# Cross-attention and quantised feed-forward on one core: the order of the work inside a tile's step

## The reference

```python
def _xattn(q1, key, value, weights, bias, drop_mask):   # key = value = ctx
    scores = jnp.einsum('bqd,bkd->bqk', q1, key) / 0.72
    attn = jax.nn.softmax(scores, axis=-1) * drop_mask
    o = jnp.einsum('bqk,bkd->bqd', attn, value) + bias
    return jnp.einsum('bqd,de->bqe', o, weights)

def _ffn(x, weight_q, weight_scale, bias):              # int8 weights, 512 x 512
    x_scale = jnp.maximum(jnp.max(jnp.abs(x), -1, keepdims=True), 1e-6) / 127.0
    x_q = jnp.clip(jnp.round(x / x_scale), -128, 127).astype(jnp.int8)
    acc = jax.lax.dot_general(x_q, weight_q, (((1,), (1,)), ((), ())), preferred_element_type=jnp.int32)
    return acc.astype(jnp.float32) * x_scale * weight_scale[None, :] + bias

x = x + _xattn(_layernorm(x), ctx, ctx, weights, attn_bias, mask)
x = x + _ffn(_layernorm(x), weight_q, weight_scale, ffn_bias)
```

## Time and profile before

| | before |
|---|---|
| median of 3 runs (lowest, highest) | 350.48 us (349.62, 350.58) |
| span of the profiled execution, first to last instruction | 348.8 us |
| PE busy | 332.0 us, 95% |
| DVE busy | 307.7 us, 88% |
| ACT busy | 239.0 us, 69% |
| POOL busy | 238.4 us, 68% |
| granted TensorE clock, mean | 0.998 |
| data moved | 43.74 MB, mean 125 GB/s |

### The profile page before, as it was taken

The page is one execution under the profiler, slowest core; times in us unless marked ns, Lnnn a source line. Parts: engine busy times, 40 slices in busy tenths (PEclk is TensorE's granted clock), DMA queues, the critical chain, the costliest instruction groups (busy, mean ns, idle before and its releaser), DMA issues. The chain is left out here.

```text
span 348.8 us, 6291 instructions
## 1 busy us (share of the span) xinstructions
PE 332.0 (95%) x1665; PEld 264.5 (76%) x1694; DVE 307.7 (88%) x630; ACT 239.0 (69%) x483; POOL 238.4 (68%) x368
## 2 busy tenths in 40 slices
PE   7999889999999999999999999999999999999993
PEld 7878667787777778777777787777778777787781
DVE  2687879989999999989999999989999999989887
ACT  3455787667777777677777667767776776777651
POOL 5163766778776777877777787867778787767643
PEclk9999999999999999999999999999999999999999
DMA  7949971634435173345516344552724341200002
GB/s 224 270 112 248 203 152 61 180 121 113 130 119 185 62 191 112 123 117 134 167 61 192 108 122 118 148 153 63 209 89 135 111 144 60 62 30 30 32 30 92
DMA packets 48226, 43.74 MB, mean 125 GB/s; under 512 B 3792, under 2 KB 34768, under 8 KB 48208
## 3 DMA queue, kind: packets, MB, share of 16 engines
q1 hardware_dynamic: 48208, 43.53, 44.6%
HBM read 35.13 MB, written 8.39 MB: 125 GB/s over the span
## 5 line engine op out<-in xcount | busy, mean ns | idle before, releaser
L1187 POOL TENSOR_TENSOR ct_lo<-ct_raw,ct_hi 128x512 fp32r<-128x512 f32 x28 | 36.3, 1296 | 29.3 <-ACT ct_hi L722 29.3
L744 ACT ACTIVATE x_norm<-x_blocks,norm_spread 128x128 f32<-128x128 f32 x124 | 51.2, 483 | 2.3 <-ACT norm_spread L737 1.5
L495 PE MATMUL ps_attn<-vw_hi,pt_hi 128*128 128x512 f32 x124 | 51.2, 413 | 0.1
L1139 POOL TENSOR_TENSOR scaled<-meanvar,scale 128x2 f32<-128x2 f32 x32 | 18.1, 564 | 46.6 <-DVE meanvar L900 46.6
L497 PE MATMUL ps_attn<-vw_hi,pt_lo 128*128 128x512 f32 x124 | 48.8, 394 | 0.0
L495 PE MATMUL ps_scores<-ct_hi,xt_hi 128*128 128x512 f32 x124 | 48.8, 393 | 0.0
L496 PE MATMUL ps_attn<-vw_lo,pt_hi 128*128 128x512 f32 x124 | 48.7, 393 | 0.0
L497 PE MATMUL ps_scores<-ct_hi,xt_lo 128*128 128x512 f32 x124 | 48.5, 391 | 0.0
L496 PE MATMUL ps_scores<-ct_lo,xt_hi 128*128 128x512 f32 x124 | 48.3, 390 | 0.0
L495 PE MATMUL ps_vw<-w_hi,ct_hi 128*128 128x512 f32 x116 | 48.2, 415 | 0.0
L497 PE MATMUL ps_vw<-w_hi,ct_lo 128*128 128x512 f32 x116 | 45.8, 395 | 0.0
(11 more groups left out here) (170 smaller groups left out, 827.4 us busy)
## 6 DMA issues: line engine op xcount, KB each, us to landing
x_in<-in_x_dram SPq DMA_DIRECT2D x32, 256.0 KB, 3.1
mask_in<-in_mask_BxSxS_fk_dram SPq DMA_DIRECT2D x32, 256.0 KB, 3.4
out_dram<-out_tile SPq DMA_DIRECT2D x31, 256.0 KB, 2.1
x_blocks<-in_x_dram SPq DMA_DIRECT2D x60, 128.0 KB, 2.9
ctx_in<-in_ctx_dram SPq DMA_DIRECT2D x56, 128.0 KB, 2.8
ctx_in<-in_ctx_dram SPq DMA_DIRECT2D x4, 256.0 KB, 4.7
x_blocks<-in_L_xattn_weights_dram SPq DMA_DIRECT2D x4, 256.0 KB, 6.5
wq_words<-in_L_ffn_weight_q_dram SPq DMA_DIRECT2D x1, 256.0 KB, 7.0
```

The source lines that it names most:

```text
L495: nc.tensor.matmul(bank_, lhs_hi(t), rhs_hi(t), start=(t == 0), stop=False)
L744: last = nc.scalar.activation(x_norm[:, k, a * P:(a + 1) * P], x_blocks[:, slot(n, 4), a * P:(a + 1) * P], ACT.Identity, bias=norm1_spread ...
L1187: nc.gpsimd.tensor_tensor(ct_lo[:, batch_of(n), :, j * P:(j + 1) * P], ct_raw[:, slot(n, 2), :, :], ct_hi[:, batch_of(n), :, j * P:(j + 1) ...
```

## The change

The order of several operations in a step is changed; no operation is added or left out.

- PE: outside the last batch the probability transposes of tile d stand ahead of the feed-forward product of tile d-2.
- ACT: outside the last batch the copy `xq_t` stands ahead of the rounding `xt_hi`.
- DVE: the score maximum stands ahead of the transpose of x (in tile 1's step it did already). The statistics of x come behind the probabilities, and their aggregation (from tile 1's step on) behind x1 of tile d-1. Outside the last batch `xt_lo` stands last of the splits, behind `pt_lo`; in the last batch it stays where it was, behind the reciprocal.
- POOL: the norm factors of tile d+3 come behind x plus bias, except in tile 0's step.

```diff
@@ PE
                     if exists(base, d - 1):
                         attend(d - 1)
+                    if not is_tile(base, d, 0):
+                        turn_probs(d)
                     if exists(base, d - 2):
                         feed_forward(d - 2)
-                    if not is_tile(base, d, 0):
-                        turn_probs(d)
@@ ACT
+                late = last_batch(base) and exists(base, d)
+                if exists(base, d - 2) and not last_batch(base):
+                    clear_integers(d - 2)
                 if exists(base, d + 1):
                     wait_count(act, xt_raw_ready, base, d + 1)
                     split_x(d + 1, flat(xt_raw[:, slot(d + 1, 2), :, :]))
                 if last_batch(base) and d > 0 and not is_tile(base, d - 2, LAST):
                     round_integers(d - 2)
-                late = last_batch(base) and exists(base, d)
-                if exists(base, d - 2) and not late:
+                if last_batch(base) and not late and exists(base, d - 2):
                     clear_integers(d - 2)
@@ DVE
-                if not is_tile(base, d, 1):
-                    turn_tiles()
+                if exists(base, d + 4) and not is_tile(base, d, 1):
+                    turn_ctx(base, d + 4)
                 if exists(base, d):
                     wait_count(dve, scores_done, base, d + 1)
...
                 if is_tile(base, d, 1):
-                    turn_tiles()
+                    turn_ctx(base, d + 4)
+                if exists(base, d + 1) and not is_tile(base, d, 0):
+                    turn_x(base, d + 1)
...
-                if exists(base, d + 3):
-                    x_statistics(base, d + 3)
...
                 if exists(base, d + 3):
-                    x_mean_var(d + 3)
+                    x_statistics(base, d + 3)
                 if exists(base, d):
                     nc.vector.reciprocal(col(inv_sum, d), col(prob_sum, d)).then_inc(inv_sum_ready, 1)
...
-                if exists(base, d + 1):
-                    split_x(base, d + 1, flat(xt_raw[:, slot(d + 1, 2), :, :]))
+                def split_next_x():
+                    if exists(base, d + 1):
+                        split_x(base, d + 1, flat(xt_raw[:, slot(d + 1, 2), :, :]))
+
+                if last_batch(base):
+                    split_next_x()
...
+                    if exists(base, d + 3):
+
+                        wait_count(dve, stats1_ready, base, d + 3 + 1)
                     nc.vector.scalar_tensor_tensor(out=x1[:, slot(n, 2), :], in0=ps_attn[:, :], scalar=col(inv_sum, n),
...
+                    if exists(base, d + 3):
+                        x_mean_var(d + 3)
...
                 if exists(base, d) and not is_tile(base, d, LAST):
                     split_probs(d)
+                if not last_batch(base):
+                    split_next_x()
@@ POOL
-                if exists(base, d + 3):
+                if exists(base, d + 3) and is_tile(base, d, 0):
                     norm_factors(base, d + 3)
...
+                if exists(base, d + 3) and not is_tile(base, d, 0):
+                    norm_factors(base, d + 3)
```

11 lines of the change are left out of this document (5 added, 6 removed).

## The result

The changed kernel takes 351.99 us (median of 20 runs, 350.21 to 354.09) against 350.39 us for the kernel before on the same chip (20 runs, 349.04 to 353.26). The ratio is 1.0045 with a 95% interval of 1.0027 to 1.0064: it is slower, by about 1.6 us. The forecast was no change, 349.8 us.

What follows compares the result with a forecast made beforehand. The prediction took PE, 95% busy, to bound the kernel. Its terms, -2.8 - 1.4 + 0.25 + 1.75 + 1.5 = -0.7 us, took the median from 350.48 to 349.8 us, with an 8-in-10 range of 347.9 to 352.2.

Steps and rivals of the forecast that it cites:

- the second gain of the steady steps: Loop, PE: the handover from float transposes to bf16 feed-forward saves 0.055 us in each of 26 steps, 1.4 us.
- Rival 3: Loop, PE: no gain at the handover between transposes and feed-forward, giving 351.2 us, still no change; chance 0.16.
- The first gain: Loop, PE: the feed-forward's wait for ACT's copy of the transposed integers goes, saving all 2.8 us lost there.
- The three late steps: Loop: in three steps with a 0.73 us gap `xt_lo` may reach the scores late; 0.25 us allowed for these.
- Sign (a): Loop: the step falls from 10.13 to 9.94 to 9.98 us, with PE's wait for the copy gone.
- Rival 2: Loop: `xt_lo` bounds the steady steps; each 0.1 us beyond its margin loses 2.5 us, giving 352.3 us; chance 0.18.
- (b): Loop, PE: probability transposes come 0.23 us behind the last attention matmul, with the feed-forward's right behind them.
- The start: First steps: `xt_lo` of tile 1 comes later, delaying its scores and what follows; 1.75 us lost.
- Sign (c): Start: tile 1's scores wait about 1.9 us for `xt_lo`; the first integer transposes come at 47.3 instead of 45.57.
- Rival 1: Start: the new wait for `xt_lo` of tile 1 is taken up by old waits, giving 348.0 us; chance 0.17.
- The last batch: Steps of tiles 28 to 30: later statistics and DVE's moved transpose of x delay PE, 1.5 us in all.
- sign (d): Last batch: integer transposes wait for ACT in the steps of tiles 29 and 30, about 0.5 and 0.7 us.

Runs made afterwards that it cites:

- e6: The changed kernel with PE's order put back (feed-forward ahead of the probability transposes); median 352.26 us, ratio 1.0038 to the kernel before.
- e7: The changed kernel with `xt_lo` back behind the reciprocal in all steps; median 351.56 us, ratio 1.0022 to the kernel before.
- e4: The kernel before with only PE's probability transposes moved ahead of the feed-forward product outside the last batch; median 348.94 us, ratio 0.9956.
- e15: The kernel before with four products of ones ahead of the bias matmuls, filling PE's idle time; median 350.13 us, ratio 1.0002.
- e2: The changed kernel with DVE's transpose of x back ahead of the maximum in the last batch; median 350.58 us, ratio 1.0003 to the kernel before.
- e10: The changed kernel with `xt_lo` behind the reciprocal everywhere, and transpose and statistics of x put back in the last batch; 349.58 us, ratio 0.9981 to the kernel before.
- e12: The changed kernel, unaltered, timed again on another chip; median 351.65 us, ratio 1.0041 to the kernel before.
- e9: The kernel before with `xq_t` ahead of `xt_hi`, and `xt_lo` behind `pt_lo` except in tile 0's step and the last batch; 348.18 us, ratio 0.9946.

## Why the prediction was wrong

**The step that failed is the second gain of the steady steps, the handover from transposes to feed-forward: -1.4 us forecast, nothing measured.** The working took 0.054 us for the step from a float transpose to a bf16 matmul, because bf16 transposes follow each other by that much. The rows above show 0.11, and in the loop the changed kernel and e6, which differ in this order alone, take 10.057 and 10.053 us a step. The two rows that I combined allow another reading, which I passed over: the transposes of float data may hold PE 0.11 us each by themselves, whatever is loaded next. Rival 3 named this case at 0.16. The Trainium skill, "TensorE: Matmul & The Clock Gate", section "LDWEIGHTS (loading the stationary operand)", gives a load of 128 columns 107 ns and makes no difference by type, and by it the gain would have been nothing. The outcome, 0.11 us, agrees with it here; the 54 ns of the bf16 transposes do not. The Trainium skill, same title, section "Weight-path perf modes — Fast Weight Load (FWL) and DoubleRow", says that loads of 128 weights that are not FP32 are faster, and gives about twice the speed as measured. The 54 ns of the bf16 transposes agree with that, beside 109 of the float ones. No run separates the load from the transpose itself.

**The first gain, -2.8 us, was right as far as the wait goes**: e7's loop, without late steps, gains 2.52 us over the 24 steps, and e4 and e6 take the wait away by one engine's order each, to the same step. **The three late steps were mis-sized**: 0.25 us for all three, measured 0.25 each (10.27 against 10.02), 0.8 with what little else differs from e7 (10.057 against 10.023 in 24 steps). The forecast had the mechanism in its text and took a third of the size, from a difference of 0.2 us per step that it had read itself. With these two the 24 steps gave -1.69, where -3.95 was said for all 25 or 26. Sign (a) fell as its own text said it would: 10.057, just at the bound of 10.06 named as the slow side. Rival 2 did not happen in the ordinary steps: `xt_lo` is in time there, as was said. Signs (b) and (e) came as forecast, 0.23 us and a maximum that waits in 31 of the steps.

**The start, +1.75 us, held within what can be read**: the profile pair shows 1.18, and counted from the second bias matmul it is 1.1 against the kernel before, 1.3 against e7 and 1.9 against e15. Sign (c) came (a wait of 1.72 us against 1.9, integers at 46.76 against 47.3). The 1.9 was a slip: scores at 31.75 with PE done at about 29.3 would have been a wait of 2.5. In parts: `xt_lo` was done 0.6 us sooner than I said, since `pt_lo` started at 29.73 instead of 30.3, so the scores start at 31.08, not 31.75, 1.97 us late instead of 2.6; and the transposes behind them are 1.07 late, since the wait ahead of them falls from 1.58 to 0.87 us. Rival 1, that all of it is taken up, is out.

**The last batch, +1.5 us, held**: 1.36, made of 0.19 (0.3 forecast), 0.55 (0.5) and 0.63 (0.7), with the waits of the integer transposes where sign (d) put them, 0.26 us each in the records and the rest in the gap before. e2 and e10 give it back, 1.2 and 1.4 us.

**What stays open**: 0.7 us between the profile pair (0.9) and the medians (1.6). They are the profiled executions: the changed kernel's was 0.54 under its median, and the one of the kernel before, at some 350.6 by its span, 0.2 over. What makes one execution slower than another is not shown. The sentence that the new idle time of PE leaves the clock alone rested on one mean, and it can't be called right or wrong: in the changed kernel's profile and in e12's the clock is whole over the idle time. 19 of 29 runs of the changed kernel have a mean grant of 0.993 or less, 32 of 124 of the kernel before, and these runs are slower in both (medians 352.3 against 351.5, and 351.7 against 350.2), but the mean does not tell where the clock was low.

**In one line**: measured by the profiles -2.5 + 0.8 + 1.2 + 1.4, with no handover gain, is +0.9 us, where -2.8 - 1.4 + 0.25 + 1.75 + 1.5 = -0.7 was said. Of the 1.6 between them 1.4 is the handover; the other four terms are off by +0.3, +0.55, -0.55 and -0.15 and nearly cancel, which is luck. The other rivals: 4 is refuted by start and end.

**What the reading of the profile missed**: it took DVE's 88% for room. In the loop of the kernel before DVE had about 0.10 us of room in a step of 10.13, in a wait too short for the list, and ACT's move without DVE's asks for 0.2 and costs 1.4 us in the loop. The prediction asked what is late next for `xt_lo` alone, and that held because the change moved `xt_lo` at the same time. Between 60 and 300 us DVE waits for PE 4.2 us ahead of x1 in e9, where `xt_lo` stands behind x1, and 7.9 us ahead of the maximum in e7, where the maximum stands ahead of the transpose. Both waits stand in the changed kernel's list, 14.4 and 7.7 us over the whole run.

## What to carry to other kernels

Read a new order stage by stage: it is written once but runs in the start, the loop and the last steps, and here one swap on one engine had as much as the whole change won in the loop, while the moves around it cost the ends more than that. A price that comes from combining two rows (this load behind that matmul) is a guess until a row has both; keep its lower end at nothing, and don't let it carry half of the gain. An engine at 88% with no wait for the bound in its list has little room: look at whom it waits for, and at the waits too short for the list, before counting its idle time as slack.
